# A graph kernel of two gather stages: SyncE fetches one piece of every second group row by row

## The chip, the cores and the metric

The kernel runs on one core of a Trainium2 chip. The metric is the time of one execution in device microseconds (us), taken as the median of several runs. The core has five engines that run side by side and meet only at semaphores: TensorE (PE, matrix products), VectorE (DVE), ScalarE (ACT), GpSimd (POOL) and SyncE (SP, which here only starts transfers). Transfers (DMAs) run on 16 DMA engines. An engine starts a transfer by an instruction in its own queue, and an engine executes its queue in order.

## What is computed

A graph has 12500 nodes with 128 features and 212500 edges. Edges are sorted by their target. Two layers follow each other; each one reads, for every edge, a row that belongs to the edge's source, and sums over the edges of a target.

```python
# h = relu(layernorm(x)); layer 0, then x = x + layer0(h)
xW = jnp.einsum('nd,rde->nre', x, W_rel)          # 8 relations: a table of 100000 rows of 128
msg = xW[src, edge_type]                          # gather 1: one row of 512 bytes per edge
agg = jax.ops.segment_sum(msg, dst, num_segments=n)
h = gelu(layernorm(agg + x @ W_self + b_conv)); x = x + h
x = x + gelu(layernorm(x) @ W1 + b1) @ W2 + b2
# h = relu(layernorm(x)); layer 1, then x = x + layer1(h)
xt = (x @ W.T + bias).reshape(n, 4, 32)           # a table of 12500 rows of 128, and 4 scores
alpha = leaky_relu(alpha_src[row] + alpha_dst[col], 0.2)
alpha = softmax of alpha over the edges of one target
out = jax.ops.segment_sum(xt[row] * alpha[..., None], col, num_segments=n)   # gather 2
```

## The kernel before

**Tables and stages.** Nodes lie in 98 blocks of 128. A first stage (to about 200 us) writes `rel_table`, one row of 512 bytes for each node and relation; SP stores it, one DMA for each block (`store_block`, L431). Gather stage 1 (about 202 to 2292 us) reads from it. While it runs, the dense part of layer 0 is worked off in quads of 4 blocks, and writes `xt_table`, one row of 528 bytes per node (128 features and 4 scores), and `x_mid`. Gather stage 2 (about 2351 to 4433 us) reads from `xt_table`.

**Groups and pieces.** The edges form 104 groups of 2048. A group fills one of four slots of the tile `G`: 128 partitions by 16 *pieces* (`CHUNKS`), and a piece is 128 rows, one for each partition. `gather` (L532 to L535) issues one indirect DMA per piece from POOL, 16 in a row for a group; it first waits that ScalarE has copied the group's row numbers into `idx`, and that the group which was in the slot has been used. `seat(g)` says which slot a group of stage 1 uses; in stage 2 it is `g % 4`. One group, the last, is taken once more by a loop over a list in each stage (`AGAIN`, the `Fori` of L550 and L570).

**Who uses a group.** In stage 1 `add_edges` (L1572) multiplies the 16 pieces on PE with a one-hot matrix (L1579, 32 instructions per group), and DVE adds the sum to `agg` (L1087). `agg_done` frees the slot. In stage 2 DVE takes the group's scores first (`scores`, L1322, needs all 16 pieces), and later multiplies the rows with the weights into `M` (L1374, three instructions; ScalarE does the last four pieces, L797). `msg_ready` and `tail_ready` free the slot.

**SyncE and ScalarE.** All queues are written out by hand. In stage 1 SP runs `store_quad` (L444 to L449): per quad it waits for `mid_ready`, stores `x_mid`, waits for `xt_sb`, and stores `xt_table`. In stage 2 it runs `store_out` (L471 to L474), one store per quad. ScalarE's stage 1 is `quad_scalar` (L749 to L768); it also copies row numbers (`load_indices`, L694), and at the next quad it waits for the store of `xt_table` (`s_xt`) anyway, since that buffer is shared. Its stage 2 is `att_scalar` with `next_indices`.

Of the kernel before, what the change touches and what calls it, by code (L numbers as in the profile page):

```python
# [13 lines left out]
P = 128  # L14
N, E, D, R, H = 12500, 212500, 128, 8, 512
# [3 lines left out]
CHUNKS = 16  # L19
# [19 lines left out]
AGAIN = 0  # L39
PARTS = 4  # L40
QUADS = -(-(BLOCKS + SHIFT) // QUAD)
LAG = 2
# [11 lines left out]
f32, bf16 = mybir.dt.float32, mybir.dt.bfloat16  # L54
i16, i32, u32 = mybir.dt.int16, mybir.dt.int32, mybir.dt.uint32
ALU = mybir.AluOpType
# [14 lines left out]
def use_of(g):  # L71

    return 1 if g < SLOTS else (g - SLOTS + 1 - (seat(g) or SLOTS)) // SLOTS + 2


# [86 lines left out]
def build(nc, x, src, dst, typ, W_rel, W_self, b_conv, g1, b1n, g2, b2n, W1, b1, W2, b2,  # L162
# [3 lines left out]
    xt_table = dram("xt_table", (BLOCKS * P, XT))  # L166
    x_mid = dram("x_mid", (P, BLOCKS, D))

    ctx = ExitStack()
    with ctx:  # L170
# [84 lines left out]
        runs = sb("runs", [P, CHUNKS])  # L255
        away = sb("away", [P, CHUNKS])


# [8 lines left out]
        typ_flat = g_flat[0:GROUPS, STORE_W + 4 * D:STORE_W + 4 * D + GROUP]  # L267
        typ_raw = typ_flat.bitcast(i32)
        by_chunk = lambda flat, c: flat.rearrange("g (p c) -> g c p", c=CHUNKS)[:, c, :]
        s_flat = agg[:, BLOCKS + 1:, :].rearrange("p b d -> p (b d)")  # L270
# [80 lines left out]
        idx_turned, state_set, c_att, c_list, c_prep = (sem(n) for n in ("idx_turned", "state_set", "c_att", "c_list", "c_prep"))  # L351
        groups, listed = Attention(sem, "group"), Attention(sem, "listed")
        rest_free, rest_idx, rest_gathered = sem("rest_free"), sem("rest_idx"), sem("rest_gathered")
        fin_done, s_out, c_fin = sem("fin_done"), sem("s_out"), sem("c_fin")
# [56 lines left out]
        def _(sp):  # L411
# [22 lines left out]
            for i in range(0, BLOCKS // STORES):  # L434
                for k in range(STORES):
                    store_block(i * STORES + k, k)
            for b in range(BLOCKS // STORES * STORES, BLOCKS):
                store_block(b, b % STORES)
            for k in range(STORES):
                sp.wait_ge(s_store[k], 16 * len(range(k, BLOCKS, STORES)) + 16)  # L440
            sp.sem_inc(tables_ready[0], 1)


# [6 lines left out]

            store_quad(0, first_of(0))
            sp.wait_ge(s_mid, 16)
            sp.wait_ge(s_xt, 16)
# [21 lines left out]

            store_out(0, first_of(0), A)
            for n in range(1, AHEAD):
                store_out(n, first_of(n), A)
            n = load_redo_count(sp)
# [11 lines left out]
        def _(pool):  # L491
# [15 lines left out]
            pool.wait_ge(s_edges, 16 * 9)  # L507
            pool_stop(pool)
            g.tensor_scalar(key_flat, src_raw, float(R), None, ALU.mult).then_inc(edges_ready, 1)
            g.tensor_copy(typ_flat, typ_raw).then_inc(edges_ready, 1)  # L510
            pool.wait_ge(edges_ready, 2)
            g.tensor_tensor(key_flat, key_flat, typ_flat, ALU.add).then_inc(edges_ready, 1)
            g.tensor_copy(dst_flat, dst_raw).then_inc(edges_ready, 1)
            g.memset(ident4[:, :, :], 0.0).then_inc(s_pool, 1)
# [16 lines left out]

            def gather(table, s, width, done):  # L532
                for c in range(CHUNKS):
                    g.indirect_dma_start(out=G[:, s, c, 0:width], out_offset=None, in_=table,  # L534
                                         in_offset=bass.IndirectOffsetOnAxis(ap=idx[:, s, c:c + 1], axis=0)).then_inc(done, 16)  # L535
# [40 lines left out]
            def att_gather(gr, s, first=False):  # L576
                pool.wait_ge(idx_ready[1], gr + 1)
                if not first:
                    pool.wait_ge(groups.msg_ready, (gr - SLOTS) * 3 + 3)
                    pool.wait_ge(groups.tail_ready, gr - SLOTS + 1)  # L580
                elif s == MAIN % SLOTS:
                    pool.wait_ge(rest_free, n + 1)
                pool_stop(pool)
                gather(xt_table, s, XT, gathered[1][s])

# [10 lines left out]
        def _(act):  # L596
# [97 lines left out]
            def load_indices(gr):  # L694

                act.wait_ge(gathered[0][seat(gr)], 16 * CHUNKS * (use_of(gr) - 1))
                a.copy(idx[:, seat(gr), :], idx_all[:, gr, :]).then_inc(idx_ready[0], 1)
# [123 lines left out]
            att_scalar(groups, 0, 0, 0)  # L821
            next_indices(1, 0, 0, 16 * CHUNKS)
            for i in range(0, (MAIN - 3) // SLOTS):
                for s in range(SLOTS):
                    gr = i * SLOTS + s + 1
                    att_scalar(groups, gr, (s + 1) % 2, (s + 1) % SLOTS)
                    next_indices(1, gr, (s + 1) % SLOTS, i * (16 * CHUNKS) + 16 * CHUNKS * (1 + (s + 1) // SLOTS))
            for gr in (MAIN - 2, MAIN - 1):
# [4 lines left out]
        def _(dve):  # L833
# [483 lines left out]
            def scores(kind, c, s, k, landed):  # L1317

                c0 = c.n
                dve.wait_ge(*landed)  # L1320
                dve_stop(dve)
# [77 lines left out]
            with dve.Fori(0, n) as i:  # L1399
# [8 lines left out]
                with dve.Fori(0, ways) as u:  # L1408
# [17 lines left out]
                    prepare(listed, c, nkey[:, :], runs[:, :], 1)  # L1426
                    scores(listed, c, slot, 1, (rest_gathered, i * (16 * CHUNKS) + 16 * CHUNKS))
                    nodes(listed, c, m, group, first)
# [12 lines left out]
            for gr in range(2):  # L1441
                prepare(groups, c, row_of(nkey_all, gr), row_of(run_all, gr), gr % 2)
            scores(groups, c, 0, 0, (gathered[1][0], 16 * CHUNKS))
            assert c.n == START
# [24 lines left out]
            c = at(0)  # L1469
            round_of(c, 0, 0, 0, first, None, (gathered[1][1], 16 * CHUNKS))  # L1470
            prepare(groups, c, row_of(nkey_all, 2), row_of(run_all, 2), 0)
            MISSED = STEPS["merge"]
            def four_rounds(i, done):

                last = load_block(dve, i * SLOTS)
                for s in range(SLOTS):
# [3 lines left out]
                    round_of(c, gr, (s + 1) % SLOTS, (s + 1) % 2, first, last,  # L1480
                             (gathered[1][(s + 2) % SLOTS], i * (16 * CHUNKS) + 16 * CHUNKS * (1 + (s + 2) // SLOTS)), done if s == 1 else None)
                    prepare(groups, c, row_of(nkey_all, gr + 2), row_of(run_all, gr + 2), (s + 1) % 2)
# [9 lines left out]
            for gr in (MAIN - 2, MAIN - 1):  # L1492
                c = Chain(dve, c_att, gr * PASS + START - MISSED - (STEPS["prep"] if gr == MAIN - 1 else 0))
                last, first = load_block(dve, gr - 1), load_block(dve, gr)
                round_of(c, gr, gr % SLOTS, gr % 2, first, last,
                         (gathered[1][(gr + 1) % SLOTS], 16 * CHUNKS * ((gr + 1) // SLOTS + 1)) if gr + 1 < MAIN else None,
                         AHEAD - 1 if gr == MAIN - 1 else None)
# [9 lines left out]
        def _(pe):  # L1507
# [63 lines left out]

            def add_edges(n, s, k, landed, picked=oh_ready, summed=agg_done):  # L1572

                pe.wait_ge(picked, n + 1)
                for c in range(CHUNKS):
                    if c % (CHUNKS // len(landed)) == 0:
                        pe.wait_ge(*landed[c * len(landed) // CHUNKS])
                        pe_stop(pe)
# [12 lines left out]
            def add_group(g):  # L1591

                landed = [(gathered[0][seat(g)], use_of(g) * (16 * CHUNKS))]
                if g == MAIN - 1:
                    landed = [(last_gathered[k], 16 * CHUNKS // PARTS) for k in range(PARTS)]
                add_edges(g, seat(g), g % 2, landed)

# [197 lines left out]
```

## Time and profile before

| | before |
|---|---|
| median of 3 runs | 4474.82 us (4474.12 to 4474.98) |
| span of the profiled execution | 4473.0 us |
| busy share of the span | POOL 71%, DVE 57%, PE 56%, ACT 19% |
| granted TensorE clock, mean | 0.737 |
| DMA engines | 23% busy, 70 GB/s over the span |

The profiled execution is known by its span, from the first to the last instruction: 4473.0 us, which is 1.8 us less than the median of the runs. Busy shares are means over stages with different limits, so a change in a stage is read from that stage. In the views of the trace a line such as `L534` is the line of the kernel, `out<-in` are its tiles, a `q` behind an engine (`SPq`) is an instruction of that engine's queue that issues a DMA or handles registers, and `<-` names what ended an idle time; `issue` is time in which the engine waited for nothing that the profile shows.

### The profile page before, as it was taken

The page shows a single profiled execution, that of the slowest core. Times are in us where ns is not written, and L with a number is a line of the kernel's source. Part 1 is how long each engine was busy: PE and PEld are TensorE (multiplying, and loading weights), DVE is VectorE, ACT ScalarE, POOL GpSimd, SP SyncE. Part 2 cuts the span into 40 slices and gives each one's busy share as a digit, 9 for nine tenths or more (in the row PEclk, how much of TensorE's full clock was granted, in tenths as well). Part 3 has the DMA queues.
Part 4 walks back from the last instruction along what each step waited for, and adds up shares of the span by engine and source line. Part 5 has one row for each costly group of instructions (what it writes and reads, how often), then busy time and mean ns, then how long its engine had stood idle before and what let it go on. Part 6 is the DMA issues. An engine that isn't in the chain of part 4 may idle for free.

```text
span 4473.0 us, 47231 instructions
## 1 busy us (share of the span) xinstructions
PE 2490.7 (56%) x13901; PEld 2075.9 (46%) x13902; DVE 2533.8 (57%) x7085; ACT 841.4 (19%) x2900; POOL 3177.0 (71%) x3356
## 2 busy tenths in 40 slices
PE   8732443434434444444445666666666666666675
PEld 3332433434333333333334555555556555565565
DVE  7741344333433334334345777777777777777777
ACT  5400110111101111011112222222222222222222
POOL 1177777777777777777737777777777777777774
PEclk9966666667667667667666777777777777777777
DMA  9622222222222222222213222222222222222221
GB/s 318 246 52 53 58 62 57 60 60 58 62 57 60 60 57 62 57 60 60 58 39 111 55 57 60 57 60 57 57 60 57 60 57 57 60 57 60 57 57 45
DMA packets 170080, 313.14 MB, mean 70 GB/s; under 512 B 58756, under 2 KB 99884, under 8 KB 169135
## 3 DMA queue, kind: packets, MB, share of 16 engines
q0 software_dynamic: 106496, 221.72, 20.7%
q1 hardware_dynamic: 47298, 81.32, 5.1%
q10 hardware_dynamic: 16034, 7.13, 0.6%
q8 instruction: 110, 1.80, 0.2%
q14 instruction: 142, 1.16, 0.1%
HBM read 238.47 MB, written 71.49 MB: 69 GB/s over the span
## 4 chain that ended last, share of the span: by engine, by line
POOL 37%; issue 29%; PE 21%; DVE 9%; ACT 2%; DMA 2%; DVEq 0%; POOLq 0%; ACTq 0%; SPq 0%
POOL G L534 37%; PE bank L1579 9%; PE quad L1624 3%; PE quad L1630 2%; DMA xt_table<-w_all 1%; PE quad L1619 1%; DVE A L1122 1%; PE quad L1527 1%; PE bank L1527 1%; PE bank L1528 1%; PE quad L1528 1%; ACT w_all L744 1%; PE quad L1666 1%; DVE stats L152 1%; PE bank L1652 1%
## 5 line engine op out<-in xcount | busy, mean ns | idle before, releaser
L534 POOL DMA_INDIRECT G<-rel_table,idx x1648 | 1564.6, 949 | 649.5 <-issue 501.7
L534 POOL DMA_INDIRECT G<-xt_table,idx x1664 | 1573.9, 946 | 566.4 <-issue 566.4
L1711 PEld LDWEIGHTS quad<-ident,top 128*128 128x128 f32 x3328 | 595.6, 281 | 273.3 <-issue 273.1
L1711 PE MATMUL quad<-ident,top 128*128 128x128 f32 x3328 | 611.8, 369 | 187.6 <-DVEq L1325 187.6
L1087 DVE SCALAR_TENSOR_TENSOR agg<-bank,sel,agg 128x128 f32 x208 | 63.5, 346 | 1039.7 <-PE bank L1579 1038.3
L1742 PE MATMUL bank<-M,onehot 128*128 128x132 f32 x3328 | 430.5, 284 | 143.4 <-DVE M L1374 139.0
L1579 PE MATMUL bank<-G,onehot 128*128 128x128 f32 x1664 | 274.1, 342 | 380.2 <-issue 367.4
L1742 PEld LDWEIGHTS bank<-M,onehot 128*128 128x128 f32 x3328 | 396.3, 193 | 175.2 <-issue 175.2
L1579 PEld LDWEIGHTS bank<-G,onehot 128*128 128x128 f32 x1664 | 270.4, 258 | 384.7 <-issue 384.7
L1579 PE MATMUL bank<-G,M 128*128 128x128 f32 x1664 | 251.4, 323 | 215.6 <-issue 200.9
L1727 PE MATMUL bank<-Z,w_all 128*128 128x8 f32 x832 | 160.0, 320 | 378.1 <-issue 372.2
L797 ACT ACTIVATE M<-G,M 128x32 f32<-128x32 f32 x1664 | 363.9, 308 | 13.6 <-ACT M L792 0.4
L1579 PEld LDWEIGHTS bank<-G,M 128*128 128x128 f32 x1664 | 245.0, 238 | 221.9 <-issue 221.9
L1727 PEld LDWEIGHTS bank<-Z,w_all 128*128 128x128 f32 x832 | 153.3, 276 | 395.3 <-issue 395.3
L1619 PE MATMUL quad<-ident,A 128*128 128x128 f32 x200 | 53.9, 424 | 503.4 <-DVE A L1122 503.4
L1619 PEld LDWEIGHTS quad<-ident,A 128*128 128x128 f32 x200 | 35.5, 215 | 511.6 <-issue 511.6
L1338 DVE TENSOR_REDUCE tops<-quad 128x4 f32<-128x2048 f32 x104 | 238.3, 2292 | 27.9 <-DVE Z L1335 17.9
L1368 DVE TENSOR_TENSOR onehot<-iota,bank 128x2048 f32<-128x2048 f32 x104 | 237.9, 2287 | 3.8
L1374 DVE TENSOR_TENSOR M<-G,bank 128x640 f32<-128x640 f32 (+1 forms) x312 | 195.8, 682 | 18.3 <-DVE onehot L1368 18.3
L1322 DVE TENSOR_TENSOR w<-G,w 128x256 f32<-128x256 f32 x104 | 63.1, 607 | 230.8 <-DMA G<-xt_table,idx 230.0
L1706 PE MATMUL quad<-ident,w_all 128*128 128x512 bf16 x416 | 181.2, 586 | 16.7 <-DVEq L1314 16.7
L786 ACT ACTIVATE fade<-fade_arg 128x8 f32<-128x8 f32 x104 | 21.7, 209 | 869.1 <-DVEq L1349 869.1
(317 smaller groups left out, 3441.8 us busy)
## 6 DMA issues: line engine op xcount, KB each, us to landing
rel_table<-G SPq DMA_DIRECT2D x98, 512.0 KB, 3.4
G<-rel_table,idx POOLq DMA_INDIRECT x1664, 2.5
G<-xt_table,idx POOLq DMA_INDIRECT x1664, 7.1
xt_table<-w_all SPq DMA_DIRECT2D x25, 264.0 KB
x_mid<-X SPq DMA_DIRECT2D x25, 256.0 KB
out<-A SPq DMA_DIRECT2D x24, 256.0 KB
x_res<-x_mid SPq DMA_DIRECT2D x3, 1792.0 KB, 15.7
x_res<-in_x ACTq DMA_DIRECT2D x11, 448.0 KB, 4.9
```

What stands on the lines that cost most here:

```text
L534: g.indirect_dma_start(out=G[:, s, c, 0:width], out_offset=None, in_=table, in_offset=bass.IndirectOffsetOnAxis(ap=idx[:, s, c:c + 1], axi ...
L797: ins = a.activation(M[:, c, hd, 0:HC], G[:, s, c, hd * HC:(hd + 1) * HC], ACT.Copy, scale=M[:, c, hd, HC:HD])
L1338: c.step(v.tensor_reduce(tops[:, :], quad[:, :].rearrange("p (j h e) -> p h j e", j=RUNS, h=HEADS), AX.XY, ALU.max))
L1368: v.tensor_tensor(onehot[:, :, :], iota1[:, :].rearrange("p (o e) -> p o e", o=1).to_broadcast([P, CHUNKS, P]), pick_key[:, k, :].rearrang ...
L1374: v.tensor_tensor(M[:, lo:hi, :, 0:HC], G[:, s, lo:hi, 0:D].rearrange("p c (h k) -> p c h k", h=HEADS), banks[7][:, lo * HEADS:hi * HEADS] ...
L1579: ins = t.matmul(banks[5 + k][:, 0:D], picks[k][:, c, :], G[:, s, c, 0:D], start=(c == 0), stop=(c == CHUNKS - 1))
L1619: ins = t.transpose(banks[0][:, j * P:(j + 1) * P], A[:, j, :], ident[:, :])
L1624: t.matmul(banks[1 + c % 2][:, :], w1[:, c * P:(c + 1) * P], tT, start=True, stop=True).then_inc(up_ps, 1)
L1706: t.matmul(banks[j][:, :], miss[:, k, j, :], ident4[:, :, :].rearrange("p h e -> p (h e)"), start=True, stop=False)
L1711: ins = t.matmul(banks[j][:, hd * P:(hd + 1) * P], top[:, j, hd:hd + 1].to_broadcast([P, P]), ident[:, :], start=False, stop=(hd == HEADS ...
L1727: ins = t.matmul(banks[5][:, j * 2 * HEADS:(j + 1) * 2 * HEADS], hit[:, j, :], Z[:, 1:3, :].rearrange("p a h -> p (a h)"), start=True, sto ...
L1742: ins = t.matmul(banks[6][:, 0:XT], onehot[:, c, :], M[:, c, :, :].rearrange("p h k -> p (h k)"), start=(c == 0), stop=(c == CHUNKS - 1))
```

## The change

In both gather stages, the groups 2, 4, ... 98 (49 of them) get only 15 pieces from POOL. The 16th piece is fetched by SP, with one plain DMA for each of its 128 rows. For that, POOL writes the byte offsets of these rows early on (`places`), SP stores them in device memory (`row_places`), and loads them back 128 at a time into `line`; one register load then fills 16 registers, and 16 DMAs follow that take their source address from one register each. The users of a group wait for one semaphore more. The stores of `x_mid`, `xt_table` and `out` of all quads but the last stand in ScalarE's queue.

```diff
+ROW_STEP = 2
+ROW_FIRST = 2
+ROW_LAST = 98
+LOADED = 16
...
+def by_rows(g):
+    return ROW_FIRST <= g <= ROW_LAST and g % ROW_STEP == ROW_FIRST % ROW_STEP
+ROWED = [g for g in range(GROUPS) if by_rows(g)]
+def pieces(g):
+    return CHUNKS - 1 if by_rows(g) else CHUNKS
...
+                if i == BLOCKS // STORES // 2:
+                    sp.wait_ge(places_ready, 2)
+                    sp.dma_start(row_places, places).then_inc(s_places, 16)
...
+            def load_line(k, m):
+                sp.dma_start(line[0:1, m % 2, :], row_places[ROWED[m]:ROWED[m] + 1, k, :]).then_inc(s_line[m % 2], 16)
+
+            def fetch_rows(k, m, slot):
+                size = row_bytes[k]
+                sp.wait_ge(s_line[m % 2], 16 * (k * len(range(m % 2, len(ROWED), 2)) + m // 2 + 1))
+                for p in range(0, P, LOADED):
+                    _, at = nc.values_load_multi_w_load_instructions(
+                        line[0:1, m % 2, p:p + LOADED], engines=[mybir.EngineType.SP], ...
+                    for j in range(LOADED):
+                        sp.dma_start(G[p + j:p + j + 1, slot, CHUNKS - 1, 0:size // 4].bitcast(u8),
+                                     table_bytes[k][bass.ds(at[j], size)].rearrange("(o b) -> o b", o=1)).then_inc(rowed[k][slot], 16)
+
+            load_line(0, 0)
+            for m, gr in enumerate(ROWED):
+                if m + 1 < len(ROWED):
+                    load_line(0, m + 1)
+                if gr >= SLOTS:
+                    sp.wait_ge(agg_done, gr - SLOTS + (2 if gr < 2 * SLOTS - 1 else 1))
+                fetch_rows(0, m, seat(gr))
...
-            for n in range(1, AHEAD):
-                store_quad(n, first_of(n))
+            store_quad(AHEAD - 1, first_of(AHEAD - 1))
...
+                if gr >= SLOTS:
+                    sp.wait_ge(groups.msg_ready, (gr - SLOTS) * 3 + 3)
+                    sp.wait_ge(groups.tail_ready, gr - SLOTS + 1)
+                fetch_rows(1, m, gr % SLOTS)
...
+            g.tensor_scalar(places[:, 1, :], by_chunk(src_raw, CHUNKS - 1), float(4 * XT), None, ALU.mult).then_inc(places_ready, 1)
...
-                gather(rel_table, seat(gr), D, gathered[0][seat(gr)])
+                gather(rel_table, seat(gr), D, gathered[0][seat(gr)], pieces(gr))
...
+                if own and not last:
+                    act.wait_ge(mid_ready, n + 1)
+                    act.dma_start(x_mid[:, bass.ds(lo, QUAD), :], X[:, :, :]).then_inc(s_mid, 16)
                 turned(n, 1, ACT.Relu)
+                if own and not last:
+                    act.wait_ge(xt_sb, n + 1)
+                    act.dma_start(xt_table.rearrange("(b p) k -> p b k", p=P)[:, bass.ds(lo, QUAD), :], xt_sbuf[:, :, :]).then_inc(s_xt, 16)
...
                 for c in range(CHUNKS):
+                    if c == CHUNKS - 1 and last is not None:
+                        pe.wait_ge(*last)
```

Three places show how the queues read now. On POOL, in stage 1 right after the loop over the list, groups 4, 5 and 6 stood so before (the first row of a group waits, the rest follow):

```order
L550 COMPARE_AND_BRANCH
L534 DMA G<-rel_table,idx 128x128 [waits idx_ready0,agg_done]
L534 DMA G<-rel_table,idx 128x128 x15
L534 DMA G<-rel_table,idx 128x128 [waits idx_ready0,agg_done]
L534 DMA G<-rel_table,idx 128x128 x15
```

and now:

```order
L623 COMPARE_AND_BRANCH
L607 DMA G<-rel_table,idx 128x128 [waits idx_ready0,agg_done]
L607 DMA G<-rel_table,idx 128x128 x14
L607 DMA G<-rel_table,idx 128x128 [waits idx_ready0,agg_done]
L607 DMA G<-rel_table,idx 128x128 x15
```

Groups 4 and 6 have one indirect DMA less, group 5 has all 16. On SP, the end of the table stage and the start of gather stage 1 were these rows:

```order
L431 DMA rel_table<-G 128x1024 [waits xwB_sb,xwA_sb] x98
L447 DMA x_mid<-X 128x512 [waits s_store3,s_store2,s_store0,s_store1,mid_ready]
L449 DMA xt_table<-w_all 128x4x132 [waits xt_sb]
L447 DMA x_mid<-X 128x512 [waits mid_ready,s_xt,s_mid]
L449 DMA xt_table<-w_all 128x4x132 [waits xt_sb]
```

and now:

```order
L467 DMA rel_table<-G 128x1024 [waits xwB_sb,xwA_sb] x52
L475 DMA row_places<-G 104x256 [waits places_ready]
L467 DMA rel_table<-G 128x1024 [waits xwB_sb,xwA_sb] x46
L488 DMA line<-row_places 1x128 [waits s_store3,s_places,s_store2,s_store0,s_store1]
L488 DMA line<-row_places 1x128
L495 TENSOR_LOAD line [waits s_line0]
L499 DMA G<-rel_table 1x512 x16
L495 TENSOR_LOAD line
L499 DMA G<-rel_table 1x512 x16
```

The pair of register load (L495) and 16 row DMAs (L499) stands eight times for each group, with no other instruction between; before the next group there is one load of the next `line` (L488). On ACT, the end of a quad in stage 1 was:

```order
L739 ACTIVATE w_all<-quad,b1col 128x512 [waits up_ps] x3
L697 CAST idx<-idx_all 128x16 [waits gathered0_0]
L730 ACTIVATE Y<-quad 128x512 [waits t_ps]
L697 CAST idx<-idx_all 128x16 [waits gathered0_1]
L744 ACTIVATE w_all<-x_res,shift_all,rstd_all 128x128 [waits s_xt]
```

and is now:

```order
L812 ACTIVATE w_all<-quad,b1col 128x512 [waits up_ps] x3
L770 CAST idx<-idx_all 128x16 [waits gathered0_0]
L843 DMA x_mid<-X 128x512 [waits mid_ready]
L803 ACTIVATE Y<-quad 128x512 [waits t_ps]
L847 DMA xt_table<-w_all 128x4x132 [waits xt_sb]
L770 CAST idx<-idx_all 128x16 [waits gathered0_1]
L817 ACTIVATE w_all<-x_res,shift_all,rstd_all 128x128 [waits s_xt]
```

Two DMAs with their waits moved in; the copy of row numbers for the next quad's first group now stands behind the wait for `xt_sb`.

## Rows read from the trace of the kernel before

**Rows 1.** Chain that ended last, from the page: shares by line.

```profile
POOL G L534 37%; PE bank L1579 9%; PE quad L1624 3%; PE quad L1630 2%; DMA xt_table<-w_all 1%; PE quad L1619 1%; DVE A L1122 1%; PE quad L1527 1%; PE bank L1527 1%; PE bank L1528 1%; PE quad L1528 1%; ACT w_all L744 1%; PE quad L1666 1%; DVE stats L152 1%; PE bank L1652 1%
```

**Rows 2.** POOL by line in 700:2200 and 2450:4400; count, busy, mean ns, idle before.

```profile
L534 POOL DMA_INDIRECT G<-rel_table,idx x1197 | 1135.3, 948 | 364.9 <-issue 364.5 <-ACT idx L697 0.3
...
L534 POOL DMA_INDIRECT G<-xt_table,idx x1560 | 1475.5, 946 | 475.5 <-issue 475.5
```

**Rows 3.** Busy time of a stretch: PE, PEld, DVE, ACT, POOL, clock, DMA share, GB/s.

```profile
1000.00:1100.00 100.00, 41.12 (x228) 35.88 (x228) 38.07 (x123) 9.14 (x21) 75.75 (x80) 0.69 0.22 58
```

**Rows 4.** SP timeline from 11 us: start, duration, instruction (the single-row issues are L422).

```profile
11.07 0.23 SPq L422 DMA_DIRECT2D M<-in_src  x1
11.34 0.68 SPq L421 DMA_DIRECT2D G<-in_edge_type  x2
12.06 0.25 SPq L422 DMA_DIRECT2D G<-in_edge_type  x1
12.35 0.76 SPq L421 DMA_DIRECT2D onehot<-in_dst  x2
```

**Rows 5.** SP issues by line: duration in ns, min/median/max, first and last start.

```profile
L422 SPq DMA_DIRECT2D M<-in_src x1: 228/228/228, 11.1 to 11.1; - x1
L422 SPq DMA_DIRECT2D G<-in_edge_type x1: 247/247/247, 12.1 to 12.1; - x1
L422 SPq DMA_DIRECT2D onehot<-in_dst x1: 252/252/252, 13.2 to 13.2; - x1
...
L431 SPq DMA_DIRECT2D rel_table<-G x98: 319/320/359, 17.4 to 198.8; - x98
...
L447 SPq DMA_DIRECT2D x_mid<-X x25: 332/332/362, 480.3 to 2336.0; - x25
...
L449 SPq DMA_DIRECT2D xt_table<-w_all x25: 382/383/389, 491.1 to 2346.9; - x25
```

**Rows 6.** Register loads on SP, one register each: duration in ns, min/median/max.

```profile
L385 SPq TENSOR_LOAD <-redo x1: 280/280/280, 2307.4 to 2307.4; - x1
...
L393 SPq TENSOR_LOAD <-redo_count x2: 278/372/467, 2306.5 to 4450.8; - x2
```

**Rows 7.** DMA queues of the whole span: packets, MB, share of 16 engines' time.

```profile
q0 software_dynamic: 106496, 221.72, 20.7%
q1 hardware_dynamic: 47298, 81.32, 5.1%
```

**Rows 8.** Waits of PE in 700:2200: total us, times, longest.

```profile
PE bank L1579 <- issue: 381.9, 37, 14.7
```

**Rows 9.** Waits of DVE in 2450:4400: total us, times, longest.

```profile
DVE w L1322 <- DMA G<-xt_table,idx: 207.2, 98, 3.0
```

**Rows 10.** Timeline, stage 1: a group on PE at its landing, and one behind dense work.

```profile
1007.39 6.43 PE L1579 MATMUL bank<-G,onehot 128*128 128x128 f32 x32 [13.80 <-issue]
...
1035.20 3.74 PE L1579 MATMUL bank<-G,M 128*128 128x128 f32 x32
```

**Rows 11.** Timeline, end of a quad in stage 1: SP's stores, ACT's next steps.

```profile
1043.02 0.33 SPq L447 DMA_DIRECT2D x_mid<-X  x1
...
1049.91 0.60 ACT L730 ACTIVATE Y<-quad 128x512 f32<-128x512 f32 x1 [15.66 <-PE quad L1619]
...
1053.89 0.38 SPq L449 DMA_DIRECT2D xt_table<-w_all  x1
...
1056.88 1.65 ACT L744 ACTIVATE w_all<-x_res,shift_all,rstd_all 128x128 f32<-128x128 f32 x4 [6.28 <-DMA xt_table<-w_all]
```

**Rows 12.** DVE timeline, stage 2: scores of two groups, and a product into M.

```profile
3012.75 0.61 DVE L1322 TENSOR_TENSOR w<-G,w 128x256 f32<-128x256 f32 x1 [0.72 <-DMA G<-xt_table,idx]
...
3032.72 0.61 DVE L1322 TENSOR_TENSOR w<-G,w 128x256 f32<-128x256 f32 x1 [2.85 <-DMA G<-xt_table,idx]
...
3040.76 1.88 DVE L1374 TENSOR_TENSOR M<-G,bank 128x256 f32<-128x256 f32 x3 [0.18 <-DVE onehot L1368]
```

**Rows 13.** POOL timeline: the first gather, and the idle time before it.

```profile
202.42 1.17 POOL L534 DMA_INDIRECT G<-rel_table,idx  x1 [147.50 <-SPq L441]
```

More of the change, by code:

```diff
@@ L73, in use_of, with seat2, fetched, rows_in @@
     return 1 if g < SLOTS else (g - SLOTS + 1 - (seat(g) or SLOTS)) // SLOTS + 2
+def by_rows(g):
[3 more added lines that the diff above has]
+    return CHUNKS - 1 if by_rows(g) else CHUNKS
+def seat2(g):
+    return g % SLOTS
+def fetched(place, g):
+    return sum(16 * pieces(k) for k in range(g + 1) if place(k) == place(g))
+def rows_in(place, g):
+    return sum(16 * P for k in ROWED if k <= g and place(k) == place(g))
 class Chain:
@@ L167, in build @@
     x_mid = dram("x_mid", (P, BLOCKS, D))
+    row_places = dram("row_places", (GROUPS, 2, P), i32)
     ctx = ExitStack()
@@ L256, in build @@
         away = sb("away", [P, CHUNKS])
+        line = sb("line", [1, 2, P], i32)
         g_flat = G[:, :, :, :].rearrange("p s a b -> p (s a b)")
@@ L268, in build @@
         typ_raw = typ_flat.bitcast(i32)
+        PLACES = STORE_W + 4 * D + GROUP
+        places = g_flat[0:GROUPS, PLACES:PLACES + 2 * P].rearrange("p (k e) -> p k e", k=2).bitcast(i32)
         by_chunk = lambda flat, c: flat.rearrange("g (p c) -> g c p", c=CHUNKS)[:, c, :]
@@ L352, in build @@
         groups, listed = Attention(sem, "group"), Attention(sem, "listed")
+        places_ready, s_places, s_line = sem("places_ready"), sem("s_places"), [sem("s_line0"), sem("s_line1")]
+        rowed = [[sem(f"rowed{k}_{i}") for i in range(SLOTS)] for k in range(2)]
         rest_free, rest_idx, rest_gathered = sem("rest_free"), sem("rest_idx"), sem("rest_gathered")
@@ L440, in _ @@
                 sp.wait_ge(s_store[k], 16 * len(range(k, BLOCKS, STORES)) + 16)
+            sp.wait_ge(s_places, 16)
             sp.sem_inc(tables_ready[0], 1)
+            table_bytes = [rel_table.rearrange("a d -> (a d)").bitcast(u8), xt_table.rearrange("a d -> (a d)").bitcast(u8)]
+            row_bytes = (4 * D, 4 * XT)
+            def load_line(k, m):
[5 more added lines that the diff above has]
+                    _, at = nc.values_load_multi_w_load_instructions(
+                        line[0:1, m % 2, p:p + LOADED], engines=[mybir.EngineType.SP], min_val=0, max_val=(BLOCKS * P * R * row_bytes[0], BLOCKS * P * row_bytes[1])[k] - size,
+                        skip_runtime_bounds_check_because="a place is a node of the inputs times the bytes of a row")
+                    for j in range(LOADED):
[8 more added lines that the diff above has]
+                fetch_rows(0, m, seat(gr))
             def store_quad(n, lo):
@@ L474, in store_out @@
                 sp.dma_start(out[bass.ds(lo * P, QUAD * P), :].rearrange("(b p) d -> p b d", p=P), tile[:, :, :]).then_inc(s_out, 16)
-            store_out(0, first_of(0), A)
-            for n in range(1, AHEAD):
-                store_out(n, first_of(n), A)
+            load_line(1, 0)
+            for m, gr in enumerate(ROWED):
+                if m + 1 < len(ROWED):
+                    load_line(1, m + 1)
+                if gr >= SLOTS:
+                    sp.wait_ge(groups.msg_ready, (gr - SLOTS) * 3 + 3)
+                    sp.wait_ge(groups.tail_ready, gr - SLOTS + 1)
+                fetch_rows(1, m, gr % SLOTS)
+            store_out(AHEAD - 1, first_of(AHEAD - 1), A)
             n = load_redo_count(sp)
@@ L512, in _ @@
             g.tensor_tensor(key_flat, key_flat, typ_flat, ALU.add).then_inc(edges_ready, 1)
+            pool.wait_ge(edges_ready, 3)
+            g.tensor_scalar(places[:, 0, :], by_chunk(key_flat, CHUNKS - 1), float(4 * D), None, ALU.mult).then_inc(places_ready, 1)
             g.tensor_copy(dst_flat, dst_raw).then_inc(edges_ready, 1)
@@ L530, in _, with gather @@
                             pattern=[[-1, P]], channel_multiplier=1).then_inc(s_pool, 1)
-            def gather(table, s, width, done):
-                for c in range(CHUNKS):
+            def gather(table, s, width, done, count=CHUNKS):
+                for c in range(count):
                     g.indirect_dma_start(out=G[:, s, c, 0:width], out_offset=None, in_=table,
@@ L583, in att_gather @@
                 pool_stop(pool)
-                gather(xt_table, s, XT, gathered[1][s])
+                gather(xt_table, s, XT, gathered[1][s], pieces(gr))
             for s in range(SLOTS):
@@ L694, in load_indices @@
             def load_indices(gr):
-                act.wait_ge(gathered[0][seat(gr)], 16 * CHUNKS * (use_of(gr) - 1))
+                act.wait_ge(gathered[0][seat(gr)], fetched(seat, gr) - 16 * pieces(gr))
                 a.copy(idx[:, seat(gr), :], idx_all[:, gr, :]).then_inc(idx_ready[0], 1)
@@ L826, in _ @@
                     att_scalar(groups, gr, (s + 1) % 2, (s + 1) % SLOTS)
-                    next_indices(1, gr, (s + 1) % SLOTS, i * (16 * CHUNKS) + 16 * CHUNKS * (1 + (s + 1) // SLOTS))
+                    next_indices(1, gr, (s + 1) % SLOTS, fetched(seat2, gr))
+                    if s == 1 and i >= LAG:
+                        act.wait_ge(fin_done, i - LAG + 1)
+                        act.dma_start(out[first_of(i - LAG) * P:(first_of(i - LAG) + QUAD) * P, :].rearrange("(b p) d -> p b d", p=P),
+                                      A[:, :, :]).then_inc(s_out, 16)
             for gr in (MAIN - 2, MAIN - 1):
@@ L1319, in scores @@
                 c0 = c.n
-                dve.wait_ge(*landed)
+                for there in landed:
+                    dve.wait_ge(*there)
                 dve_stop(dve)
@@ L1426, in _ @@
                     prepare(listed, c, nkey[:, :], runs[:, :], 1)
-                    scores(listed, c, slot, 1, (rest_gathered, i * (16 * CHUNKS) + 16 * CHUNKS))
+                    scores(listed, c, slot, 1, [(rest_gathered, i * (16 * CHUNKS) + 16 * CHUNKS)])
                     nodes(listed, c, m, group, first)
@@ L1442, in _, with landed_in @@
                 prepare(groups, c, row_of(nkey_all, gr), row_of(run_all, gr), gr % 2)
-            scores(groups, c, 0, 0, (gathered[1][0], 16 * CHUNKS))
+            def landed_in(gr):
+                there = [(gathered[1][gr % SLOTS], fetched(seat2, gr))]
+                return there + [(rowed[1][gr % SLOTS], rows_in(seat2, gr))] if by_rows(gr) else there
+            scores(groups, c, 0, 0, landed_in(0))
             assert c.n == START
@@ L1469, in _ @@
             c = at(0)
-            round_of(c, 0, 0, 0, first, None, (gathered[1][1], 16 * CHUNKS))
+            round_of(c, 0, 0, 0, first, None, landed_in(1))
             prepare(groups, c, row_of(nkey_all, 2), row_of(run_all, 2), 0)
@@ L1495, in _ @@
                 round_of(c, gr, gr % SLOTS, gr % 2, first, last,
-                         (gathered[1][(gr + 1) % SLOTS], 16 * CHUNKS * ((gr + 1) // SLOTS + 1)) if gr + 1 < MAIN else None,
+                         landed_in(gr + 1) if gr + 1 < MAIN else None,
                          AHEAD - 1 if gr == MAIN - 1 else None)
@@ L1569, in _, with add_edges @@
             t.matmul(banks[2][:, 128:128 + ng], spanc[:, 4:5].to_broadcast([ng, P]), ident[0:ng, 0:ng], start=True, stop=True).then_inc(s_setpe, 1)
-            def add_edges(n, s, k, landed, picked=oh_ready, summed=agg_done):
+            def add_edges(n, s, k, landed, picked=oh_ready, summed=agg_done, last=None):
                 pe.wait_ge(picked, n + 1)
                 for c in range(CHUNKS):
+                    if c == CHUNKS - 1 and last is not None:
+                        pe.wait_ge(*last)
+                        pe_stop(pe)
                     if c % (CHUNKS // len(landed)) == 0:
@@ L1591, in add_group @@
             def add_group(g):
-                landed = [(gathered[0][seat(g)], use_of(g) * (16 * CHUNKS))]
+                landed = [(gathered[0][seat(g)], fetched(seat, g))]
                 if g == MAIN - 1:
                     landed = [(last_gathered[k], 16 * CHUNKS // PARTS) for k in range(PARTS)]
-                add_edges(g, seat(g), g % 2, landed)
+                add_edges(g, seat(g), g % 2, landed, last=(rowed[0][seat(g)], rows_in(seat, g)) if by_rows(g) else None)
             for g in range(2):
```

10 lines of the change are left out of this document (4 added, 6 removed).

## The prediction

> **What bounds the kernel now.** I read first the chain that ended last, by line. It names L534, the indirect gather on POOL, with 37% of the span [rows 1]; no other line has a tenth. Then I asked what POOL does in each gather stage. The reader is to see the two numbers of a line together, busy time and the idle time ahead of it: in 700 to 2200 us 1197 pieces take 1135.3 + 364.9 us, which is 1.253 us for each, and in 2450 to 4400 us 1560 pieces take 1475.5 + 475.5, which is 1.251 us [rows 2]. The idle time is called "issue": 0.3 us between two pieces, in which POOL waits for nobody. So both stages run at 16 x 1.25 = 20.0 us per group, and POOL alone sets that. In a stretch of stage 1 POOL is busy for 75.75 us of 100, with 80 pieces, while PE and DVE have about 40 [rows 3].
>
> Then I asked whether the others could go faster. In stage 1 PE sat idle ahead of L1579 for 381.9 us, twice in each of 19 quads [rows 8]: 20 us per quad of 80. In stage 2 DVE waited 207.2 us for gathered rows in 98 rounds [rows 9], 2.1 us per round; it could run at 17.9 us per group. So POOL's time can fall by some per cent before another engine takes over.
>
> **What goes.** Of 49 groups in each stage POOL issues 15 pieces, not 16. That takes away 49 x 1.253 + 49 x 1.251 = 122.7 us of POOL's queue, all of it on the path. Two groups together then take POOL 31 x 1.25 = 38.75 us, where it was 40.0. PE and DVE can follow: four groups come in 77.5 us, the dense part has 20 us to spare per quad, and DVE needs 4 x 17.9 = 71.6.
>
> **What comes, and decides.** SP has to fetch 128 rows for each second group. If it needs a time T for them, and T is at most 38.75 us, the whole 122.7 us are gained; above that SP sets the pace, at T per two groups. With 49 such pairs in each of two stages the change then costs 98 x (T - 40.0) us, and at T = 40 nothing is won. So the sum for T is what matters.
>
> - *One row.* The nearest rows are three DMAs that SP issued for a single row [rows 5]: 228, 247 and 252 ns. From start to start they took 0.27 us (11.07 to 11.34) and 0.29 us (12.06 to 12.35) [rows 4]. Those have a fixed address. Lines that are issued with a fixed address 24 times and once, in a loop, with one from a register, show what that adds: the median and the largest are 332 and 362 ns for L447, 382 and 389 for L449 [rows 5], so 7 to 30 ns. The bounds for a row are 0.27 + 0.007 = 0.277 us and 0.29 + 0.03 = 0.32 us. I take the low end, since an issue that is repeated sits at its minimum: 98 stores of L431 have 319, 320 and 359 ns [rows 5]. 128 rows: 35.5 us (high end 41.0).
> - *Register loads.* There are 8 for a group, each for 16 registers. The trace has only loads of one register: 278 to 280 ns on SP, 467 for one of them [rows 6]. Low bound: 16 neighbouring words cost as one, 8 x 0.28 = 2.2 us. High bound: 16 times as much, 8 x 16 x 0.28 = 35.8 us. I take the low one, as it is the only duration that a row shows for one such instruction; it is the weakest step.
> - *The next line of places.* One issue of a single row, 0.28 us. Its landing is hidden, because it is issued one group ahead.
>
> T = 35.5 + 2.2 + 0.3 = 38.0 us. That is under 38.75 by 0.7 us only, 2% of T.
>
> **The other parts cost nothing, and here is their cover.**
> - *Time to land.* SP may start on a slot when the group in it has been used. In stage 2 a group whose scores were taken at 3012.75 is out of its slot at 3040.76 + 1.88 = 3042.64 [rows 12]. The scores of the slot's next group come four groups later, at 3012.75 + 77.5 = 3090.25. So there are 47.6 us for T and the landing; a store's median landing is 3.4 us, which gives 41.4. In stage 1 a group leaves its slot at 1013.8 when PE takes it at once, or at 1038.9 when it stood behind dense work, some 12 us after its landing [rows 10], and 65 us are left. Without that cover SP would wait for the slot, and T would grow by what is missing.
> - *DMA engines.* Stores on SP's queue have 5.1% of 16 x 4473 us for 47298 packets [rows 7], 77 ns each. If a single row stays on one engine, with one packet for its data and one for the semaphore, 256 packets load that engine with 19.8 us. The gathers put 20.7% x 16 x 4473 / 106496 = 139 ns on each of their packets, two per piece and engine, 31 x 0.28 = 8.6 us. Together 28.4 of 38.75 us, so even then there is room.
> - *Stores on ScalarE.* Two issues per quad, 0.33 and 0.38 us [rows 11], on an engine that is busy for 9 us of 100 [rows 3]. The wait for mid_ready (store at 1043.0) is over before ACT's next step at 1049.9, and ACT waited for the store of xt_table until 1056.9 in any case [rows 11]. What now stands behind the wait for xt_sb (1053.9) is a copy of row numbers that ran at 1050.4; POOL needs it three groups later. In stage 2 DVE's finish comes ahead of the scores of its round, so ACT finds fin_done set.
> - *Setup.* POOL sat idle for 147.5 us until the tables were stored [rows 13]; two small products and the store of the places fit there.
>
> Sum: the profiled span becomes 4473.0 - 122.7 = 4350.3 us. The median of the runs lies 1.8 us above the span shown, so I predict **4352 us**.
>
> **The rivals.**
> 1. *A row costs SP more than I took; SP becomes the bound, and the kernel is slower.* For it: the middle values, 0.28 + 0.018, give 38.1 us for the rows alone, and T = 40.6 with the loads; and the bounds are from issues that stood alone, whereas here 128 follow each other. Against it: the repeated stores at their minimum. It decides from T = 40.0 on, which is 0.293 us for a row. T = 41.5 gives 4475 + 147 = 4622 us, the high end (41.0 + 2.2 + 0.3 = 43.5) gives 4475 + 343 = 4818.
> 2. *A register load costs by the number of registers.* At 16 times 0.28 us, T = 35.5 + 35.8 + 0.3 = 71.6 us, and 98 x 31.6 is 3097 us more: 7572. Half of that price per register gives T = 53.7 and 5818. It decides from (40.0 - 35.8)/8 = 0.52 us for a load of 16. For it: no row shows more than one register; against it: nothing in the trace shows that it does grow. The Trainium skill has such a rule: its page "Runtime: NRT & Kernel Launch", section "Instruction fetch mechanics", says that a register load takes some 200 ns for each register, in bulk too. No run here shows that yet; by it the sum would be an estimate of T = 35.5 + 8 x 3.2 + 0.3 = 61.4 us, and 6570 us in all. The same skill's page "DMA: Bandwidth & Descriptors", section "Latency and other measured facts", gives 600 ns as the least for such a load; the trace has 280 ns, so here the measurement decides.
> 3. *SP ends between: T of 38.8 to 39.8.* Part of the gain is lost: T = 39.4 gives 4475 - 59 = 4416.
> 4. *One stage does not follow.* If the dense chain of stage 1, whose order on PE and DVE is fixed, held at 80 us per quad, only 61.3 us would be gained: 4413. Against it are the two waits per quad [rows 8].
>
> That the change doesn't do what it says I leave out: the rows of the queues show 15 pieces and 8 x 16 single rows.
>
> **How the numbers follow.** The forecast of a full gain has 0.46: the sum says yes, with a margin of 2% and one price that is only bounded. Rival 3 has 0.04 and rival 4 0.03, both faster. T close to 40, where nothing can be told from no change (within 0.2%, 9 us, about what a measurement of this kernel can tell), has 0.04. Rival 1 has 0.28 and rival 2 0.15. Faster: 0.46 + 0.04 + 0.03 = 0.53; the same: 0.04; slower: 0.43. The range leaves out rival 2 and the uppermost sixth of rival 1, together 0.20: from 4345, a little under the full gain, to 4800 us. The forecast's own range is 4345 to 4420.
>
> **What would show it.** In the profile after, POOL's line should have 49 pieces fewer in each stage, still at 1.25 us and with idle time of 0.3 us that is called issue. SP's row issues should stand 0.28 us apart, and a load of 16 registers should take about 0.3 us, with SP waiting now and then for a slot. If POOL waits ahead of the first piece of a group for agg_done, or for msg_ready, and PE or DVE wait for transfers of single rows, SP is the bound, and I am wrong. The distance of two L499 then tells whether the row or the load did it.

## The result, and the profile after

The changed kernel takes 5662.8 us (5659.8 to 5667.1, 4 runs) against 4474.9 us; the ratio is 1.266, with a 95% interval of 1.264 to 1.267. It is 1188 us slower. The forecast of 4352 us had the wrong direction, and the measured time lies far above the range: rivals 1 and 2 came together, rival 1 at its high end (a row at 0.32 us) and rival 2 at some 30% of its high price (8 loads at 10.6 us, where 35.8 was the bound).

The chain that ended last, by engine and by line, from the page of the kernel after:

```profile
SPq 74%; issue 17%; PE 4%; DVE 4%; DMA 0%; POOL 0%; DVEq 0%; ACT 0%; POOLq 0%; ACTq 0%
SPq L499 56%; SPq L495 17%; PE quad L1617 1%; PE bank L1617 1%; PE bank L1618 1%; PE quad L1618 1%; SPq L488 0%; PE bank L1672 0%; DVE onehot L1452 0%; DVE tops L1422 0%; POOL G L607 0%; PE quad L1717 0%; DVE M L1458 0%; PE quad L1804 0%; DVE run_all L1095 0%
```

Where POOL's gather stood with 37% [rows 1], there are now SP's row DMAs (L499) and its register loads (L495), with 73% between them. The SP timeline in stage 1 shows the pace. A line of this view is either the load of the next line of places, or the 128 row DMAs of a group with the register loads among them:

```profile
1048.50 0.24 SPq L488 DMA_DIRECT2D line<-row_places  x1
1050.09 51.20 SPq L499 DMA_DIRECT2D G<-rel_table  x128
1101.35 0.24 SPq L488 DMA_DIRECT2D line<-row_places  x1
```

From 1048.50 to 1101.35 is T = 52.85 us for a group, where 38.0 was forecast and 38.75 allowed. The views by line give the pieces of it (ns, min/median/max):

```profile
L495 SPq TENSOR_LOAD <-line x784: 1132/1229/1807, 202.7 to 5537.9; - x196
...
L499 SPq MOVE G<-rel_table x6272: 29/29/29, 203.9 to 2793.5; - x196
L499 SPq DMA_DIRECT2D G<-rel_table x6272: 227/228/367, 204.0 to 2793.6; - x196
```

A row DMA has the 228 ns that were taken from the smallest of [rows 5]. But each is preceded by a MOVE of 29 ns, which the queue's listing did not show. The chain of the same kernel, from 1061.15 us on, shows what stands from one row to the next:

```profile
1061.15 0.23 SPq L499
1061.38 0.04 issue
1061.42 0.03 SPq L499
1061.45 0.03 issue
1061.48 0.23 SPq L499
1061.70 0.04 issue
1061.74 1.23 SPq L495
```

DMA, gap, MOVE, gap, DMA: from 1061.15 to 1061.48 some 0.32 us. So 128 rows take 41.0 us, and 8 loads with their gaps 8 x 1.33 = 10.6 us. The line of places and the first rows behind each load, which take a little longer, are the rest. The others wait for SP. First POOL's gathers by line, in 700:2600 and in 3100:5400 (count, busy, mean ns, idle time before them and what ended it):

```profile
L607 POOL DMA_INDIRECT G<-rel_table,idx x1113 | 1052.0, 945 | 849.0 <-issue 706.1 <-PE bank L1672 137.7 <-ACT idx L770 5.2
...
L607 POOL DMA_INDIRECT G<-xt_table,idx x1357 | 1282.6, 945 | 1018.5 <-DVE M L1458 610.6 <-issue 402.4 <-ACT idx L754 5.5
```

Then the waits of PE in 700:2700 and of DVE in 3100:5400 (us in total, times, longest):

```profile
PE bank L1672 <- DMA G<-rel_table: 918.3, 38, 40.5
...
DVE w L1406 <- DMA G<-xt_table: 738.2, 44, 17.9
```

One indirect DMA still has 945 ns, as before [rows 2], but POOL now idles 849 us of 1900 in stage 1. Some 334 us of that are its usual gaps of 0.3 us. The rest comes in waits of some 7 to 15 us at the first piece of a group, where POOL's queue waits for `agg_done`; the profile names PE for only a part of them and calls the others "issue". In stage 2 it names DVE's product, which frees the slot, for 610.6 us. So POOL waits for slots, and the slots wait for single rows. At each second group PE stands for up to 40.5 us ahead of its last piece, and DVE up to 17.9 us ahead of the scores.

With T the whole time can be worked out, in a sum that was made after the result. In a stage SP fetches 49 groups back to back. In the time in which it does that, POOL used to gather 100 groups (0 to 98, and the last one in the loop over the list) at 20.0 us. So a stage grows by 49 T - 2000 us, 590 us at T = 52.85: 4474.9 + 1180 = 5655 us, against 5662.8 measured. By stages the profiles grew by 581 us up to POOL's first gather of stage 2 (2351.1 to 2931.7 us) and by 605 us behind it, so each stage is met within 15 us only.

### The profile page after: what moved, and what is told of

Read it like the earlier page. It is cut to its first block, busy times and chain, and to the rows that moved or that the text cites. A ratio compares the mean times of both kernels' runs of the same rounds, so it can differ in the third digit from the quotient of the medians.

```text
span 5658.1 us, 73253 instructions
## 1 busy us (share of the span) xinstructions
PE 2468.1 (44%) x13901; PEld 2051.9 (36%) x13902; DVE 2544.7 (45%) x7085; ACT 838.7 (15%) x2900; POOL 3076.8 (54%) x3260
## 4 chain that ended last, share of the span: by engine, by line
SPq 74%; issue 17%; PE 4%; DVE 4%; DMA 0%; POOL 0%; DVEq 0%; ACT 0%; POOLq 0%; ACTq 0%
SPq L499 56%; SPq L495 17%; PE quad L1617 1%; PE bank L1617 1%; PE bank L1618 1%; PE quad L1618 1%; SPq L488 0%; PE bank L1672 0%; DVE onehot L1452 0%; DVE tops L1422 0%; POOL G L607 0%; PE quad L1717 0%; DVE M L1458 0%; PE quad L1804 0%; DVE run_all L1095 0%
## 5 line engine op out<-in xcount | busy, mean ns | idle before, releaser
L607 POOL DMA_INDIRECT G<-xt_table,idx x1615 | 1526.5, 945 | 1253.2 <-DVE M L1458 653.0
L607 POOL DMA_INDIRECT G<-rel_table,idx x1599 | 1513.1, 946 | 1214.3 <-issue 902.1
L1804 PE MATMUL quad<-ident,top 128*128 128x128 f32 x3328 | 591.0, 360 | 800.2 <-DVEq L1409 799.8
L1804 PEld LDWEIGHTS quad<-ident,top 128*128 128x128 f32 x3328 | 577.0, 273 | 883.7 <-issue 882.9
L1672 PEld LDWEIGHTS bank<-G,onehot 128*128 128x128 f32 x1664 | 244.2, 233 | 1166.6 <-issue 1166.6
L1835 PE MATMUL bank<-M,onehot 128*128 128x132 f32 x3328 | 448.2, 291 | 156.4 <-DVE M L1458 152.1
L876 ACT ACTIVATE M<-G,M 128x32 f32<-128x32 f32 x1664 | 363.8, 307 | 13.3
L1672 PE MATMUL bank<-G,M 128*128 128x128 f32 x1664 | 229.8, 305 | 57.7 <-issue 43.0
L803 ACT ACTIVATE Y<-quad 128x512 f32<-128x512 f32 x50 | 29.9, 597 | 1496.5 <-PE quad L1712 1496.5
L1672 PEld LDWEIGHTS bank<-G,M 128*128 128x128 f32 x1664 | 227.2, 223 | 58.6 <-issue 58.6
L1712 PEld LDWEIGHTS quad<-ident,A 128*128 128x128 f32 x200 | 35.5, 215 | 516.5 <-issue 516.5
L870 ACT ACTIVATE bank<-z 128x64 f32<-128x64 f32 x104 | 23.7, 228 | 1269.9 <-DVEq L1449 1269.9
L1458 DVE TENSOR_TENSOR M<-G,bank 128x640 f32<-128x640 f32 (+1 forms) x312 | 195.7, 682 | 18.3 <-DVE onehot L1452 18.3
```

The lines of the kernel that those rows point to most:

```text
L876: ins = a.activation(M[:, c, hd, 0:HC], G[:, s, c, hd * HC:(hd + 1) * HC], ACT.Copy, scale=M[:, c, hd, HC:HD])
L1458: v.tensor_tensor(M[:, lo:hi, :, 0:HC], G[:, s, lo:hi, 0:D].rearrange("p c (h k) -> p c h k", h=HEADS), banks[7][:, lo * HEADS:hi * HEADS] ...
L1672: ins = t.matmul(banks[5 + k][:, 0:D], picks[k][:, c, :], G[:, s, c, 0:D], start=(c == 0), stop=(c == CHUNKS - 1))
L1804: ins = t.matmul(banks[j][:, hd * P:(hd + 1) * P], top[:, j, hd:hd + 1].to_broadcast([P, P]), ident[:, :], start=False, stop=(hd == HEADS ...
L1835: ins = t.matmul(banks[6][:, 0:XT], onehot[:, c, :], M[:, c, :, :].rearrange("p h k -> p (h k)"), start=(c == 0), stop=(c == CHUNKS - 1))
```

## The experiments

Two theories stood against each other. **Theory A**: SP's issue time is the bound, as a plain sum of row issues and register loads. **Rival B**: the row transfers themselves, small ones on few DMA engines, or their landing, limit the pace. A second question was whether the slots add a bound of their own (A2 against A1).

**fixed_rows.** The register loads are taken out, and each row has a fixed address.

```diff
-                    _, at = nc.values_load_multi_w_load_instructions(...)
...
-                                     table_bytes[k][bass.ds(at[j], size)].rearrange("(o b) -> o b", o=1)).then_inc(rowed[k][slot], 16)
+                                     table_bytes[k][(p + j) * size:(p + j + 1) * size].rearrange("(o b) -> o b", o=1)).then_inc(rowed[k][slot], 16)
```

> The 128 single-row transfers per group stay, but each takes its source from a fixed address, and the register loads are gone; so the 16th piece of the 49 groups holds other rows than the edges ask for. Theory A (SyncE's issue time sets the pace): a row falls from 0.32 us to 0.27 us and the loads (8 x 1.33 us) go, so a group takes SyncE 128 x 0.27 + 0.3 = 34.9 us, less than GpSimd's 38.75 us; full gain, 4352 us. Rival B (the transfers themselves, all of one row and on few DMA engines, or their landing set the pace): the same transfers are left, about 5660 us.

Measured: 4351.8 us, ratio 0.973 (0.971 to 0.974). The same number of single-row DMAs, 12544, costs nothing when SP can issue them fast enough. They read the same 128 rows each time, so this run alone doesn't show that rows from all over the table are as harmless. Other profiles do: in the changed kernel transfers have 0% of the chain that ended last, and in step3 the true rows of stage 2 that stand on that chain land 1.2 to 1.8 us after their issue. With that, B falls. The SP timeline of this kernel, and behind it SP's issues by line (ns, min/median/max):

```profile
1031.86 0.25 SPq L488 DMA_DIRECT2D line<-row_places  x1
1032.32 38.17 SPq L496 DMA_DIRECT2D G<-rel_table  x128
1070.54 0.25 SPq L488 DMA_DIRECT2D line<-row_places  x1
```

```profile
L496 SPq DMA_DIRECT2D G<-rel_table x6272: 214/252/419, 202.0 to 2116.5; - x196
```

POOL waits for nothing but its own issue in stage 2 of this kernel (2700:4300):

```profile
POOL G L604 <- issue: 391.2, 1282, 0.3
```

T is 38.68 us, 0.07 us under POOL's 38.75. But a row takes 38.17/128 = 0.298 us, not the 0.27 us that was expected here from two starts of [rows 4]: back to back, the median of a DMA with a fixed address is 252 ns, the largest and not the smallest of [rows 5]. The full gain stood on a margin of 0.07 us, where 3.9 us had been expected.

**fixed_rows_loads.** The intent was to keep the loads beside rows with fixed addresses.

> As fixed_rows (other rows than the edges ask for), but the 8 register loads per group are still issued, and nobody uses the registers. Theory A: 128 x 0.27 + 8 x 1.33 + 0.9 = 46.1 us per group on SyncE, 98 x 6.1 = 598 us over 4475: about 5070 us. If the address from a register (the MOVE ahead of each row) is the whole loss and loads are hidden: 4352 us. If the loads are the whole loss: about 5660 us.

Measured: 4351.1 us. This tells nothing of the loads: nobody read the registers, and no TENSOR_LOAD from `line` is in the trace. It is a second run of fixed_rows.

**one_of_16.** The same with the first of each 16 rows taking its address from the load, which keeps the loads in the program.

```diff
-                                     table_bytes[k][bass.ds(at[j], size)].rearrange(...)
+                                     (table_bytes[k][bass.ds(at[j], size)] if j == 0 else table_bytes[k][(p + j) * size:(p + j + 1) * size]).rearrange(...)
```

> As fixed_rows, but the first of each 16 rows takes its address from the register load again, so that the 8 loads per group are really issued (in fixed_rows_loads nobody used the registers, and the loads had been left out of the program); 15 of 16 rows are other rows than the edges ask for. A fixed row was measured at 0.30 us from start to start, a load of 16 registers with its gaps at 1.33 us. Theory A (issue times add up on SyncE): 38.7 + 8 x 1.33 = 49.3 us per group, and 0.2 us for 8 addresses from a register: 98 x 9.5 = 931 us over 4475, about 5400 us. If loads run beside the rows: about 4352 us.

Measured: 5298.8 us, ratio 1.183 (1.181 to 1.186). The loads do not run beside the rows; they add up. The SP timeline, and the loads by line:

```profile
1041.63 0.25 SPq L488 DMA_DIRECT2D line<-row_places  x1
1043.25 47.75 SPq L499 DMA_DIRECT2D G<-rel_table  x128
1091.04 0.25 SPq L488 DMA_DIRECT2D line<-row_places  x1
```

```profile
L495 SPq TENSOR_LOAD <-line x784: 1132/1226/1871, 202.1 to 5177.2; - x196
```

T = 49.41 us was expected as 49.5. Against fixed_rows that is 10.7 us more for 8 loads, 1.34 us each. The changed kernel differs from this one only in 120 of the 128 addresses, which come from registers there, and needs 3.44 us more for a group (52.85 against 49.41), some 0.03 us for each. The time came out 101 us lower than expected; 80 us of that are SP's start, two groups ahead in each stage, which 98 x (T - 40) left out. With 49 T - 2000 per stage it is 4478 + 842 = 5320 us; the last 21 us stay unexplained.

**load_8.** `LOADED = 16` becomes 8: twice as many loads, each half as long.

> Register loads of 8 instead of 16 registers, twice as many. Theory A with a price per load that is part fixed, part per register (one register 0.28 us, 16 registers 1.23 us, so 0.063 us for each further one): 16 x (0.72 + 0.10) = 13.1 us against 10.6 us per group, 98 x 2.5 = 245 us slower than the changed kernel, about 5900 us. If a load costs by the number of registers alone: no difference, 5660 us. If it costs the same for any number: 16 x 1.33 = 21.3 us, about 6700 us.

Measured: 5988.3 us, ratio 1.338 (1.336 to 1.341), 326 us above the changed kernel, where 245 was expected. The loads by line:

```profile
L495 SPq TENSOR_LOAD <-line x1568: 684/783/1375, 202.2 to 5866.7; - x196
```

One register takes 280 ns at best [rows 6], 8 take 783, 16 take 1229: each further one costs some 0.06 us, and an instruction has a fixed part of some 0.2 to 0.3 us. The price by number alone and the price that is the same for any number both fall. The straight line between 1 and 16 registers was only rough: it gave 0.72 us for 8. With the 0.78 us measured, 16 loads come to 1 us more for a group and some 100 us more in all, about what was missing to 326 us.

**step3.** `ROW_STEP = 2` becomes 3.

> Every third group is fetched by rows (2, 5, ... 98: 33 groups), in both stages. Three groups take GpSimd 58.75 us, SyncE needs 52.85 us for one. Theory A1 (only SyncE's pace counts): GpSimd is the bound again, 2 x 33 x 1.25 = 82 us less than before, 4393 us. Theory A2 (pace, and in stage 2 the slot too: it comes free 9.9 us after the scores of the last row-fetched group, then 52.85 us of issues and 1.5 us of landing): stage 2 runs at 64.2 us per three groups instead of 60, +140 us, stage 1 still gains 41 us: about 4574 us.

Measured: 4547.0 us, ratio 1.016 (1.014 to 1.018), 27 us under A2's 4574. A2 holds: one group in three leaves SP enough time in sum, and yet the kernel is 1.6% slower than before. In the profile stage 1 is 40.5 us shorter, where 41 was forecast, and stage 2 is 113 us longer, where 140 was forecast. SP's timeline in stage 2, then its waits in 2400:4400 (us in total, times, longest), then DVE's timeline:

```profile
3092.09 0.24 SPq L488 DMA_DIRECT2D line<-row_places  x1
3104.63 51.14 SPq L499 DMA_DIRECT2D G<-xt_table  x128
3155.82 0.24 SPq L488 DMA_DIRECT2D line<-row_places  x1
```

```profile
SPq L493 <- ACT M L876: 311.4, 32, 18.5
SPq L495 <- DVE M L1458: 48.9, 32, 1.5
```

```profile
3093.35 0.61 DVE L1406 TENSOR_TENSOR w<-G,w 128x256 f32<-128x256 f32 x1 [7.89 <-DMA G<-xt_table]
3101.49 1.88 DVE L1458 TENSOR_TENSOR M<-G,bank 128x256 f32<-128x256 f32 x3 [0.18 <-DVE onehot L1452]
...
3157.16 0.61 DVE L1406 TENSOR_TENSOR w<-G,w 128x256 f32<-128x256 f32 x1 [10.39 <-DMA G<-xt_table]
```

SP waits about 11 us for each slot, first for the part that ScalarE multiplies (L876) and then for DVE's product (L1458). It issues for 51 us, and the scores follow some 1.4 us after its last issue: 63.7 us from 3092.09 to 3155.82, where POOL needs 58.75. The slot comes free with the product that ends at 3103.4, and that product stands behind the scores of the last row-fetched group (3093.35). So the loop closes on itself.

**no_rows.** No group is fetched by rows; what is left of the change are the stores on ScalarE and the places.

```diff
 def by_rows(g):
-    return ROW_FIRST <= g <= ROW_LAST and g % ROW_STEP == ROW_FIRST % ROW_STEP
+    return False
```

> No group is fetched by rows; the dense stores and the stores of the output stay on ScalarE, and the places are still worked out and stored. Theory A: that part costs nothing, 4475 us, no difference from before. Rival: the stores on ScalarE hold its queue up, some us per quad, 24 quads and 23 stores of the output: 4500 us or more.

Measured: 4477.7 us against 4478.3 us, ratio 1.000 (0.999 to 1.001): that part costs nothing, as forecast.

**first3 and first3_second7.** Each stage has a step of its own: 3 and none, then 3 and 7.

```diff
-ROWED = [g for g in range(GROUPS) if by_rows(g)]
+STEPS_OF = (3, 7)
+def by_rows(k, g):
+    return STEPS_OF[k] > 0 and ROW_FIRST <= g <= ROW_LAST and g % STEPS_OF[k] == ROW_FIRST % STEPS_OF[k]
+ROWED = [[g for g in range(GROUPS) if by_rows(k, g)] for k in range(2)]
```

> Every third group in stage 1 only (33 groups), none in stage 2. Theory A2: 33 x 1.253 = 41 us off before, 4433 us; a slot of stage 1 is free early enough for 52.85 us of issues. If the dense chain of stage 1 holds: 4475 us.

> Every third group in stage 1 and every seventh in stage 2 (14 groups). Theory A2: in stage 2 the rows of a group come about 5 us late after the slot is free, VectorE has some 2 us to spare per group and has caught up long before the next such group, so GpSimd keeps its pace: 41 + 14 x 1.251 = 59 us off before, 4416 us. If each late group costs its 5 us for good: 14 x 5 - 17 = 53 us more than first3, about 4487 us.

Measured: 4434.9 us, ratio 0.990 (0.989 to 0.992), and 4418.8 us, ratio 0.987 (0.985 to 0.989). That is 43 us off before for the first, where some 41 was forecast, and 59 us for the second, where 59 was. These two are faster than the kernel before, by 1.0% and 1.3%, and the second is the fastest that computes the whole. DVE's waits in stage 2 of first3_second7 (2500:4400), and all of POOL's waits for its gathers of more than a few us:

```profile
DVE w L1413 <- DMA G<-xt_table,idx: 99.3, 51, 3.3
DVE w L1413 <- DMA G<-xt_table: 78.6, 13, 7.0
...
POOL G L614 <- issue: 1055.8, 3264, 60.6
POOL G L614 <- SPq L486: 146.1, 1, 146.1
```

The 13 waits for single rows, 6 us each, are there, but POOL never waits for a slot: its two long waits stand ahead of the first gathers of the two stages. VectorE makes the time up from the 2.1 us per round that it has to spare [rows 9].

## Why the prediction was wrong, point by point

- *POOL sets 20.0 us per group, and the others can follow:* right. With the rows cheap enough (fixed_rows) the time was 4351.8 us, against 4352 forecast, 122.6 us off before for the term of 122.7.
- *One row at 0.277 us: the step that failed first.* It measured 0.32 us, which is the upper bound that was given, though by another sum: the bound put 30 ns on a longer issue, whereas the issue stayed at 228 ns and a MOVE with a gap came on top. That the two agree is luck. I had taken the smallest of three durations, with the argument that repeated issues sit at their minimum. For a fixed address they did not: 252 ns, 0.298 us from start to start. With an address from a register the DMA does take 228 ns, but a MOVE and a second gap come with each. The trace of before had it too, beside the one store in a loop whose address came from a register, and I compared only the durations of the DMAs. This term: 41.0 us for 35.5 us. The row that I passed over, from the view of L447 of the kernel before:

```profile
L447 SPq MOVE x_mid<-X x1: 29/29/29, 2335.9 to 2335.9; - x1
```

- *A register load of 16 at 0.28 us: the step that failed worse.* It measured 1.23 us, 1.33 us with its gaps: 10.6 us for 2.2. With the row's 5.5 us these 8.4 us make nearly all of the 14.9 us between the T that was forecast and the one measured. The point of decision, 0.52 us a load, was in the text; the value taken was the low end of a range from 2.2 to 35.8 us, only since one row showed it. Even that row was the best of few: of the four loads of one register on SP in the trace of before, two took 278 and 280 ns and two 467 and 564. By the sum for T each of the two errors alone was enough to make the kernel slower (T = 43.5 with the row alone, 46.4 with the loads alone). Rival 2 was right that a load grows with its registers. The Trainium skill's page "Runtime: NRT & Kernel Launch", section "Instruction fetch mechanics", gives some 200 ns for each register; here, for loads from the on-chip tile `line`, each further register measured some 60 ns.
- *A margin of 0.7 us on a sum that was made of low ends:* the chance of 0.46 was too high for it. Middle values for the row alone, before any price per register, gave T = 40.6. By the prediction's own rule that is 59 us slower than before, and by 49 T - 2000 some 20 us faster; nearly all of the gain is gone either way. Rivals 1 and 2 were treated as alternatives, and both came, which no case held.
- *98 x (T - 40.0):* right in form, some 80 us too much for both stages together: 49 row-fetched groups stand in for 100 groups of POOL and not for 98.
- *DMA engines have room:* right, fixed_rows shows it. *Stores on ScalarE and setup at nothing:* right, no_rows shows it. *Time to land and slots:* at T = 38.7 in fixed_rows SP waited for slots for some 48 us in the whole run, and POOL lost nothing by it; at T = 52.85 the pace decided first. The bound is real, though: of 58.75 us per three groups step3 leaves a slot free for 48.7 us (the product ends 10.0 us after the scores), close to the 47.6 worked out for the kernel as it was forecast, and issues and landing of 54 us do not fit.
- *What would show it:* POOL waiting for agg_done and msg_ready, PE and DVE for transfers of single rows, was named as the sign that SP is the bound, and is what the profile after shows, for POOL with the waits that the profile puts down to "issue". The distance of two L499 was to tell whether the row or the load did it; both did.

## What to carry to other kernels

Where work moves from a slow queue to another that has to issue it piece by piece, the forecast is the new queue's time per piece, and that is the distance from one start to the next with all that comes along (address moves, gaps, register loads), not the duration of the issue. When a sum is within a few per cent of its limit and some of its prices are only bounded, take middles, and let the bounds add up in one case. And a helper that is fast enough on average can still lose to the time between a buffer coming free and its next use.

## What the runs showed of the hardware that was not expected

- A DMA of one row issued back to back has a median of 252 ns on SP with a fixed address, and 228 ns with one from a register, which has a MOVE of 29 ns and a gap of 0.03 us ahead of it; from start to start 0.298 against 0.32 us.
- A register load on SP takes 280 ns for one register at best (two of four loads; the others 467 and 564), and at the median 783 ns for 8 and 1229 for 16. The row DMAs behind it don't start meanwhile: 8 loads of 16 made a group 10.7 us longer.
- 12544 DMAs of one row beside the gathers took nothing from POOL: in fixed_rows its pieces stayed at 944 to 948 ns and its gaps at 0.3 us.
